# Pair stage of an attention and mixture-of-experts block: layer 2 in seven PSUM banks, rows straight from the projection, one layer-3 count a batch

## Chip, cores and metric

The kernel runs on one core of one Trainium2 chip. The metric is the device time of the whole program in microseconds (us), lower is better. Before the change the median of three runs is 1792.36 us (1785.63 to 1807.71).

## The reference

The input x is 16 batches of 256 tokens of width 256. After a layer norm it goes through a sparse attention and a routed and a shared feed-forward part, and all are added to x. The stage that the change touches decides, for every pair (i, j) of tokens of a batch, how similar they are; the 25 most similar j of each i are then the only ones that i attends to:

```
h    = xn @ W1.T                                  # 128 features a token
pair = relu(h[:, :, None, :] - h[:, None, :, :] + b1)   # for each i, j: 128 values
pair = relu(einsum('bijf,gf->bijg', pair, W2) + b2)     # layer 2: 64 values
sim  = einsum('bijg,og->bijo', pair, W3)[..., 0] + b3   # layer 3: one value
sim  = 0 on the diagonal; top_idx = top 25 of each row of sim
```

All of it is in float32. The attention (32 heads of width 2) gathers keys and values of the 25 chosen tokens; the feed-forward part sends each of the 4096 tokens to 2 of 8 experts.

## The kernel before

The program has three stages. The first (until about 96 us) makes the layer norms, the projections h, q, k and v and the routing logits, batch by batch. For all batches it leaves in SBUF `h_both`: `hneg`, which is -h, and `hb`, which is h + b1, both as 128 features x 4096 tokens. The second, the pair stage (about 96 to 1408 us), is the subject. The third (to 1787 us) runs the experts and the shared part.

The pair stage has 16 batches of 32 steps (`BSTEPS`), 512 in all, numbered n. A step takes 8 tokens i of a batch against all 256 tokens j. Its parts, each in a function that an engine's program calls in order:

- **Rows** (`relu1_row` on VectorE, L1338; `relu1` on ScalarE, L1093): for each of the 8 tokens one instruction makes relu(-h[:, j] + (h + b1)[:, i]) for all 256 j, a "row" of 128 x 256. `dve_rows(s)` says how many of the 8 VectorE makes (2 to 7; 148 in a batch), the rest (108 in a batch) is ScalarE's. Rows go to `r1`, a ring of four steps: rows of step n wait for layer 2 of step n-4.
- **Layer 2** (`layer2`, L905, TensorE): the 8 rows times W2, four matmuls of 512 columns, two at a time on the two halves of the PSUM partitions; each is recorded as two instructions, so a step has 8 records. The result fills two PSUM banks. There are three such pairs of banks (0 to 5), so layer 2 of step n waits until the ReLU of step n-3 has read its pair (`r2_done`).
- **Layer-2 ReLU** (`relu2`, L1141, ScalarE): one instruction of 128 x 1024 from the two banks to `r2`, a ring of eight steps in SBUF. It waits for layer 2 of its step (`l2_done`) and, since `r2` is used again, for a layer-3 group (`l3_done`). ScalarE does the rows of step n and then the ReLU of step n-3 (`LAG`).
- **Layer 3** (`layer3`, L917, TensorE): after every second step, four matmuls of 512 columns on four partition groups; 16 groups in a batch add into bank 6 (`ps_sim`). Each group increments `l3_done`.

VectorE takes the finished sums at step 5 of the next batch (`take_sims`, L1454), finds the top 25 in four rounds (steps 6 to 10 of each half batch) and does the attention's arithmetic between the rows. GpSimd (POOL) gathers keys and values with indirect DMAs (L734) whose turns are paced by `l2_done`. ScalarE makes the exponentials (L1145), two a batch.

The rows don't read `h_both` in place. At step 17 (`COPY`) of each batch VectorE copies the next batch's 2 x 256 columns to one of two SBUF buffers `h_now` (`copy_batch`, L1329), and at step 20 (`MOVE`) ScalarE copies the -h half of it on into PSUM bank 7 (`move_next`, L1128). ScalarE's rows of batches 1 to 15 read -h from there, and those of batch 0 from `h_now` in SBUF; VectorE's rows always read `h_now`.

The order of work on each engine is written out by hand; semaphores alone tie the engines together. SP (the DMA queue of the sync engine) waits for the last copy (`batch_copied`, in batch 14) and then loads the first experts' weights (L547 to L553) over `h_both`; POOL splits those of expert 0 (L742, L744) after its gathers in batch 15. The third stage starts with transposes (`transpose_slots`, L961) into banks 7 and 4, then 6 and 7 in turn.

Of the kernel before, what the change touches and what calls it, by code (L numbers as in the profile page):

```python
# [5 lines left out]
def lsn_attention_moe_block(  # L6
# [24 lines left out]
    ALU = mybir.AluOpType  # L31
    ACT = mybir.ActivationFunctionType
    AX = mybir.AxisListType.X
    ds = bass.ds
# [53 lines left out]
    with ctx:  # L88
# [73 lines left out]
        h_now = [part(2 * S, 2), sb("h_now1", [P, 2, S])[:, :, :]]  # L162
        hneg_now, hb_now = ([h[:, k:k + 1, :].rearrange("p o n -> p (o n)") for h in h_now] for k in range(2))
# [112 lines left out]
        ps_before = ps[:, 7, 0:NT * E].rearrange("p (t e) -> p t e", e=E)  # L276
        ps_count = ps[:, 7, NT * E:2 * NT * E].rearrange("p (t e) -> p t e", e=E)
# [65 lines left out]
        batch_copied = sem("batch_copied")  # L343
        batch_moved = sem("batch_moved")
# [70 lines left out]
        COPY, MOVE = 17, 20  # L415
# [4 lines left out]


# [45 lines left out]
        def _(sp):  # L467
# [72 lines left out]
            sp.wait_ge(batch_copied, NB)  # L540
# [46 lines left out]
            for g in range(ALL):  # L587
# [6 lines left out]
                if g == SWUG_LOAD:  # L594
                    sp.wait_ge(l3_done, NB * GROUPS)
# [231 lines left out]
        def _(pe):  # L827
# [61 lines left out]
            def count_choices():  # L889
# [3 lines left out]
                nc.tensor.matmul(ps[:, 7, 0:NT * E], earlier[:, :], hv, start=True, stop=True)  # L893
                nc.tensor.matmul(ps[:, 7, NT * E:2 * NT * E], ones[:, :], hv, start=True, stop=True).then_inc(counts_ready, 1)

            def layer2(n):
# [3 lines left out]
                if n >= PS2:  # L900

                    pe.wait_ge(r2_done, n - PS2 + 1)
                for u in range(2):
                    for v in range(2):
                        last = nc.tensor.matmul(ps_l2(n)[v * G2:(v + 1) * G2, u, :], w2t[:, :],  # L905
# [3 lines left out]
            def layer3(b, q):  # L909
# [6 lines left out]
                for c in range(4):  # L916
                    last = nc.tensor.matmul(ps[32 * c:32 * c + 32, 6, :], w3win[:, at:at + 32],  # L917
                                            r2[:, (2 * q + c // 2) % R2, 512 * (c % 2):512 * (c % 2) + 512],
                                            start=(q == 0), stop=(q == GROUPS - 1))
                last.then_inc(l3_done, 1)  # L920
# [146 lines left out]
        def _(act):  # L1067
# [13 lines left out]
            def relu1(b, i, s, first):  # L1081
# [4 lines left out]
                if s == 0:  # L1086
# [700 lines left out]
```

## Time and profile before

| | us |
|---|---|
| runs | 1807.71, 1785.63, 1792.36 |
| profiled execution, its time | 1788.49 |
| span from its first to its last instruction | 1786.8 |
| TensorE busy in the span | 1664.4 (93%) |
| VectorE busy | 1523.8 (85%) |
| ScalarE busy | 1441.1 (81%) |
| GpSimd busy | 1125.6 (63%) |
| mean granted TensorE clock | 0.991 |

The profiled execution lies 4 us under the median of the runs. Busy shares are averages over three stages; matmul ends are modelled, so that busy time of TensorE (PE) is not time at its peak. A wait is shown as idle time before an instruction, with what ended it; "remote" (or "another core or an unknown queue") stands where the profile finds no event that fits. Starts of neighbouring instructions in a timeline give what one costs its engine; the recorded duration is longer, since the end of one lies over the start of the next.

### The profile page before, as it was taken

The page shows a single profiled execution, that of the slowest core. Times are in us where ns is not written, and L with a number is a line of the kernel's source. Part 1 is how long each engine was busy: PE and PEld are TensorE (multiplying, and loading weights), DVE is VectorE, ACT ScalarE, POOL GpSimd, SP SyncE. Part 2 cuts the span into 40 slices and gives each one's busy share as a digit, 9 for nine tenths or more (in the row PEclk, how much of TensorE's full clock was granted, in tenths as well). Part 3 has the DMA queues.
Part 4 walks back from the last instruction along what each step waited for, and adds up shares of the span by engine and source line. Part 5 has one row for each costly group of instructions (what it writes and reads, how often), then busy time and mean ns, then how long its engine had stood idle before and what let it go on. Part 6 is the DMA issues. An engine that isn't in the chain of part 4 may idle for free.

```text
span 1786.8 us, 30738 instructions
## 1 busy us (share of the span) xinstructions
PE 1664.4 (93%) x9092; PEld 722.8 (40%) x9092; DVE 1523.8 (85%) x4205; ACT 1441.1 (81%) x2787; POOL 1125.6 (63%) x1027
## 2 busy tenths in 40 slices
PE   7999979999998999899999999998999999998998
PEld 6732212222222222222222222222222599997887
DVE  6898948979998998889899898998899688867888
ACT  5699948989998999899899989998899787843342
POOL 3207766767676777767676767777676634455556
PEclk9999979999999999999999999999999999999999
DMA  5622111111111111111111111111121166532333
GB/s 184 249 83 82 54 51 42 45 45 48 45 49 39 50 45 46 47 43 51 42 48 45 49 42 48 49 44 48 52 82 40 57 196 211 172 125 72 118 118 106
DMA packets 80074, 136.88 MB, mean 77 GB/s; under 512 B 22336, under 2 KB 46528, under 8 KB 79936
## 3 DMA queue, kind: packets, MB, share of 16 engines
q0 software_dynamic: 31744, 69.27, 14.0%
q1 hardware_dynamic: 48192, 65.91, 11.1%
q8 instruction: 70, 1.15, 0.3%
q14 instruction: 68, 0.56, 0.1%
HBM read 95.24 MB, written 39.85 MB: 76 GB/s over the span
## 4 chain that ended last, share of the span: by engine, by line
PE 36%; ACT 36%; DVE 9%; issue 8%; another core or an unknown queue 4%; DMA 0%; SPq 0%; ACTq 0%; DVEq 0%
ACT arena L1093 21%; PE ps L905 16%; PE ps L944 16%; ACT arena L1141 13%; DVE arena L1338 4%; PE ps L917 4%; PE ps L961 1%; DVE arena L1512 1%; ACT arena L1145 1%; DVE idx L1469 1%; DVE top L1462 0%; DVE hTs_low L1694 0%; DVE arena L1482 0%; DVE arena L1468 0%
## 5 line engine op out<-in xcount | busy, mean ns | idle before, releaser
L734 POOL DMA_INDIRECT arena<-kv_rows,gidx x800 | 887.2, 1109 | 437.8 <-issue 226.2
L905 PE MATMUL ps<-arena,w2t 128*64 128x512 f32 x4096 | 982.5, 603 | 86.5 <-ACT arena L1141 51.1
L1141 ACT ACTIVATE arena<-ps,b 128x1024 f32<-128x1024 f32 x512 | 633.9, 1242 | 133.7 <-remote 90.2
L905 PEld LDWEIGHTS ps<-arena,w2t 128*64 128x64 f32 x4096 | 281.2, 136 | 777.9 <-issue 668.7
L1338 DVE TENSOR_SCALAR arena<-h_now 128x256 f32<-128x256 f32 x1184 | 388.1, 384 | 78.1 <-remote 45.2
L1338 DVE TENSOR_SCALAR arena<-arena 128x256 f32<-128x256 f32 x1184 | 377.1, 375 | 53.1 <-PE ps L905 26.5
L1093 ACT ACTIVATE arena<-ps,h_now 128x256 f32<-128x256 f32 x864 | 382.1, 632 | 0.0
L1093 ACT ACTIVATE arena<-ps,arena 128x256 f32<-128x256 f32 x756 | 326.5, 600 | 0.0
L917 PE MATMUL ps<-arena,w3win 128*32 128x512 f32 x2048 | 275.7, 606 | 1.4 <-issue 1.2
L917 PEld LDWEIGHTS ps<-arena,w3win 128*32 128x32 f32 x2048 | 40.8, 108 | 211.1 <-issue 162.9
L1512 DVE TENSOR_TENSOR arena<-arena 128x1152 f32<-128x1152 f32 (+4 forms) x160 | 100.2, 626 | 0.4
L815 POOL DMA_INDIRECT arena<-slot_outputs,slot_get x64 | 70.3, 1099 | 29.1 <-issue 16.6
L687 POOL DMA_INDIRECT slot_inputs<-arena,slot_put x36 | 39.5, 1098 | 63.7 <-issue 48.5
L1253 ACT ACTIVATE off_diag<-ps 128x512 f32<-128x512 f32 (+1 forms) x24 | 14.3, 595 | 77.7 <-PE ps L944 36.6
L944 PE MATMUL ps<-xTe_high,wug_high 128*112 128x256 f32 (+1 forms) x240 | 70.6, 294 | 0.0
L944 PE MATMUL ps<-xT_high,swug_low 128*128 128x512 f32 x176 | 69.1, 393 | 1.3 <-issue 1.3
L944 PE MATMUL ps<-xT_high,swug_high 128*128 128x512 f32 x176 | 70.0, 398 | 0.2 <-DVE off_diag L1688 0.2
L944 PE MATMUL ps<-xT_low,swug_high 128*128 128x512 f32 x176 | 69.2, 393 | 0.0
L944 PE MATMUL ps<-xTe_low,wug_high 128*112 128x256 f32 (+1 forms) x240 | 67.5, 281 | 0.0
L944 PE MATMUL ps<-xTe_high,wug_low 128*112 128x256 f32 (+1 forms) x240 | 67.3, 281 | 0.0
L1482 DVE TENSOR_TENSOR arena<-arena,qao 128x1600 f32<-128x1600 f32 x32 | 58.3, 1822 | 6.9 <-issue 5.1
L663 POOL TENSOR_TENSOR arena<-arena 128x2 f32<-128x2 f32 x32 | 23.9, 763 | 62.1 <-DVE arena L1302 62.1
(158 smaller groups left out, 2115.7 us busy)
## 6 DMA issues: line engine op xcount, KB each, us to landing
arena<-kv_rows,gidx POOLq DMA_INDIRECT x800
slot_inputs<-arena SPq DMA_DIRECT2D x16, 640.0 KB, 3.9
arena<-slot_inputs SPq DMA_DIRECT2D x40, 256.0 KB
slot_outputs<-arena SPq DMA_DIRECT2D x40, 256.0 KB
arena<-in_L_attn_x_dram SPq DMA_DIRECT2D x16, 256.0 KB, 3.0
xn_rows<-arena SPq DMA_DIRECT2D x16, 256.0 KB, 3.8
arena<-in_L_attn_x_dram SPq DMA_DIRECT2D x8, 512.0 KB
arena<-xn_rows SPq DMA_DIRECT2D x8, 512.0 KB
```

The lines of the kernel that those rows point to most:

```text
L663: nc.gpsimd.tensor_tensor(rstd[:, r, :], veps[:, r, :], neg_half, ALU.pow).then_inc(rstd_ready[r], 1)
L687: pool.indirect_dma_start(out=slot_dram, out_offset=bass.IndirectOffsetOnAxis(ap=slots, axis=0), in_=rows, in_offset=None, bounds_check=SL ...
L734: pool.indirect_dma_start(out=kvg[:, h, r, :], out_offset=None, in_=kv_dram, in_offset=bass.IndirectOffsetOnAxis(ap=gidx[:, h, r:r + 1], a ...
L815: pool.indirect_dma_start(out=ys[c % 2][:, n, k, :], out_offset=None, in_=yslot_dram, in_offset=bass.IndirectOffsetOnAxis(ap=slot_get[:, c ...
L905: last = nc.tensor.matmul(ps_l2(n)[v * G2:(v + 1) * G2, u, :], w2t[:, :], r1[:, n % R1, 4 * u + 2 * v:4 * u + 2 * v + 2, :], start=True, s ...
L917: last = nc.tensor.matmul(ps[32 * c:32 * c + 32, 6, :], w3win[:, at:at + 32], r2[:, (2 * q + c // 2) % R2, 512 * (c % 2):512 * (c % 2) + 512],
L944: mm = nc.tensor.matmul(to, weights[a], moving[b], start=(first and i == 0), stop=(last_one and i == 2))
L1093: last = nc.scalar.activation(r1[:, n % R1, k, :], hneg_now[i] if first else ps_hneg[i], ACT.Relu, bias=hb_now[i][:, at:at + 1])
L1141: nc.scalar.activation(r2[:, n % R2, :].rearrange("p (u n) -> p u n", u=2), ps_l2(n), ACT.Relu, bias=b2[:, 0:1]).then_inc(r2_done, 1)
L1338: row = nc.vector.tensor_scalar(r1[:, (b * BSTEPS + s) % R1, k, :], hneg_now[i], hb_now[i][:, at:at + 1], 0.0, ALU.add, ALU.max)
L1482: nc.vector.tensor_tensor(prod, kvg[:, h, :, 0:KD], qao[:, ds(t, 1), :].to_broadcast([P, TOPK, KD]), ALU.mult)\
L1512: nc.vector.tensor_tensor(pve[:, 0:n, :], pve[:, 0:n, :], pve[:, rows - n:rows, :], ALU.add).then_inc(attn_step, 1)
```

## The change

Three things change in the pair stage, and three places follow from them. Layer 2 takes its banks from a table: steps 0 to 15 use three pairs as before, and from step 16 on a step's two halves take the next two of seven banks (0 to 6) in turn. A half waits only for the ReLU that last read its own bank, and the half that is free earlier goes first. Where the two banks are not neighbours (6 and 0), the ReLU is two instructions of 512 columns. The sums move to bank 7. Rows read `h_both` in place, and only the last batch is copied, once, since the experts' weights land on the original. Layer 3 increments `l3_done` once a batch, and the ReLU no longer waits for it. SP waits for the last copy and for the rows of batch 14 before it loads weights. The first transposes use banks 0 and 2.

```diff
-        h_now = [part(2 * S, 2), sb("h_now1", [P, 2, S])[:, :, :]]
-        hneg_now, hb_now = ([h[:, k:k + 1, :].rearrange("p o n -> p (o n)") for h in h_now] for k in range(2))
+        h_last = part(2 * S, 2)
...
-        PS2 = 3
-
-        def ps_l2(n):
-            return ps[:, 2 * (n % PS2):2 * (n % PS2) + 2, :]
-
-        ps_hneg = [ps[:, 7, i * S:(i + 1) * S] for i in range(2)]
-
-        ps_sim = ps[:, 6, :].rearrange("p (h n) -> p h n", h=HALVES)
+        SIM, RING2 = 7, 7
+
+        def l2_banks(n):
+
+            if n < STEPS:
+                return (2 * (n % 3), 2 * (n % 3) + 1)
+            half = 2 * (n - STEPS) + 2
+            return tuple(sorted((half % RING2, (half + 1) % RING2)))
+
+        l2_free, bank_user = [], {}
+        for n in range(NB * BSTEPS):
+            l2_free.append([bank_user.get(k, -1) + 1 for k in l2_banks(n)])
+            bank_user.update({k: n for k in l2_banks(n)})
+
+        def ps_l2(n, u):
+            return ps[:, l2_banks(n)[u], :]
+
+        ps_sim = ps[:, SIM, :].rearrange("p (h n) -> p h n", h=HALVES)
...
         def ps_xt(g):
-            bank = (7, 4)[g] if g < 2 else 6 + g % 2
+            bank = (0, 2)[g] if g < 2 else 6 + g % 2
...
+        def h_rows(b, k):
+
+            h = h_both[:, k:k + 1, b * S:(b + 1) * S] if b < NB - 1 else h_last[:, k:k + 1, :]
+            return h.rearrange("p o n -> p (o n)")
...
-            sp.wait_ge(batch_copied, NB)
+            sp.wait_ge(last_copied, 1)
+            sp.wait_ge(r1_dve, (NB - 1) * BSTEPS)
+            sp.wait_ge(r1_act, (NB - 1) * BSTEPS)
...
                 pe.wait_ge(r1_dve, n + 1)
                 pe.wait_ge(r1_act, n + 1)
-                if n >= PS2:
-
-                    pe.wait_ge(r2_done, n - PS2 + 1)
-                for u in range(2):
+                for u in sorted(range(2), key=lambda u: l2_free[n][u]):
+                    if l2_free[n][u]:
+
+                        pe.wait_ge(r2_done, l2_free[n][u])
                     for v in range(2):
...
-                last.then_inc(l3_done, 1)
+                if q == GROUPS - 1:
+                    last.then_inc(l3_done, 1)
...
-                if g == 1:
-
-                    pe.wait_ge(r2_done, NB * BSTEPS - 2)
+                if g < 2:
+
+                    pe.wait_ge(r2_done, NB * BSTEPS - 3 + g)
                 if g == 2:
+
+                    pe.wait_ge(r2_done, NB * BSTEPS)
+                if g == 3:
 
                     pe.wait_ge(sim_taken, NB)
...
-                    last = nc.scalar.activation(r1[:, n % R1, k, :], hneg_now[i] if first else ps_hneg[i], ACT.Relu,
-                                                bias=hb_now[i][:, at:at + 1])
+                    last = nc.scalar.activation(r1[:, n % R1, k, :], h_rows(b, 0), ACT.Relu, bias=h_rows(b, 1)[:, at:at + 1])
...
-            def move_next(b, i, first):
-
-                act.wait_ge(batch_copied, b + 2)
-                if first:
-                    act.wait_ge(route_done, 1)
-                nc.scalar.activation(ps_hneg[1 - i], hneg_now[1 - i], ACT.Copy).then_inc(batch_moved, 1)
...
-                if n >= R2:
-
-                    act.wait_ge(l3_done, (n - R2) // 2 + 1)
-                nc.scalar.activation(r2[:, n % R2, :].rearrange("p (u n) -> p u n", u=2), ps_l2(n), ACT.Relu, bias=b2[:, 0:1]).then_inc(r2_done, 1)
+                low, high = l2_banks(n)
+                pair = r2[:, n % R2, :].rearrange("p (u n) -> p u n", u=2)
+                if high == low + 1:
+                    nc.scalar.activation(pair, ps[:, low:high + 1, :], ACT.Relu, bias=b2[:, 0:1]).then_inc(r2_done, 1)
+                else:
+                    for u in range(2):
+                        last = nc.scalar.activation(pair[:, u, :], ps_l2(n, u), ACT.Relu, bias=b2[:, 0:1])
+                    last.then_inc(r2_done, 1)
...
-            def copy_batch(b, i):
-
-                nc.vector.tensor_copy(h_now[i], h_both[:, :, ds(b * S, S)]).then_inc(batch_copied, 1)
+            def copy_last():
+
+                nc.vector.tensor_copy(h_last, h_both[:, :, (NB - 1) * S:NB * S]).then_inc(last_copied, 1)
...
-                row = nc.vector.tensor_scalar(r1[:, (b * BSTEPS + s) % R1, k, :], hneg_now[i], hb_now[i][:, at:at + 1], 0.0, ALU.add, ALU.max)
+                row = nc.vector.tensor_scalar(r1[:, (b * BSTEPS + s) % R1, k, :], h_rows(b, 0), h_rows(b, 1)[:, at:at + 1], 0.0, ALU.add, ALU.max)
```

## Rows read from the trace of the kernel before

**Rows 1.** The page, part 1: busy us, share of the span, instructions of each engine.

```profile
PE 1664.4 (93%) x9092; PEld 722.8 (40%) x9092; DVE 1523.8 (85%) x4205; ACT 1441.1 (81%) x2787; POOL 1125.6 (63%) x1027
```

**Rows 2.** Windows, batches 0, 1, 2-14, 15: us, then PE, PEld, DVE, ACT, POOL busy us.

```profile
96.31:171.22 74.91, 72.94 (x374) 20.09 (x375) 67.89 (x283) 74.49 (x142) 28.60 (x24) 1.00 0.20 69
171.22:271.39 100.17, 84.47 (x387) 20.80 (x383) 68.77 (x187) 71.28 (x141) 69.79 (x66) 0.90 0.17 53
...
271.39:1332.49 1061.10, 991.76 (x4994) 261.75 (x4994) 952.18 (x2759) 960.05 (x1861) 752.90 (x677) 1.00 0.17 48
1332.49:1408.30 75.81, 74.96 (x387) 19.70 (x384) 62.67 (x194) 72.38 (x139) 47.14 (x41) 1.00 0.14 37
```

**Rows 3.** Timeline of TensorE, late batch 15: start us, us, engine, line, operation.

```profile
1378.88 3.65 PE L905 MATMUL ps<-arena,w2t 128*64 128x512 f32 x16
...
1383.46 3.65 PE L905 MATMUL ps<-arena,w2t 128*64 128x512 f32 x16
```

**Rows 4.** Timeline of ScalarE, batch 7: a ReLU, six rows from PSUM, a ReLU.

```profile
748.69 1.20 ACT L1141 ACTIVATE arena<-ps,b 128x1024 f32<-128x1024 f32 x1
749.69 2.39 ACT L1093 ACTIVATE arena<-ps,h_now 128x256 f32<-128x256 f32 x6
751.83 1.26 ACT L1141 ACTIVATE arena<-ps,b 128x1024 f32<-128x1024 f32 x1
```

**Rows 5.** Timeline of ScalarE, batch 14: the copy into PSUM and an exponential.

```profile
1300.45 0.51 ACT L1128 ACTIVATE ps<-h_now 128x256 f32<-128x256 f32 x1
1300.76 1.24 ACT L1141 ACTIVATE arena<-ps,b 128x1024 f32<-128x1024 f32 x1
...
1330.77 1.18 ACT L1145 ACTIVATE arena<-arena 128x800 f32<-128x800 f32 x1
1331.53 0.78 ACT L1093 ACTIVATE arena<-ps,h_now 128x256 f32<-128x256 f32 x1
```

**Rows 6.** Waits in 94 to 1411 us: who <- whom: us in total, times, longest.

```profile
PE ps L905 <- ACT arena L1141: 51.1, 70, 3.8
...
ACT arena L1141 <- remote: 90.2, 36, 16.8
```

**Rows 7.** Timelines of TensorE, ScalarE and VectorE at a pause in batch 4.

```profile
450.34 1.94 PE L905 MATMUL ps<-arena,w2t 128*64 128x512 f32 x8
...
452.89 2.46 ACT L1093 ACTIVATE arena<-ps,arena 128x256 f32<-128x256 f32 x6
457.02 1.11 ACT L1141 ACTIVATE arena<-ps,b 128x1024 f32<-128x1024 f32 x1 [1.67 <-remote]
...
457.03 0.35 DVE L1338 TENSOR_SCALAR arena<-arena 128x256 f32<-128x256 f32 x1 [0.30 <-remote]
```

**Rows 8.** The chain of waits by line: batches 2 to 14, then batch 15.

```profile
by line: ACT arena L1093 30.8%; PE ps L905 19.5%; ACT arena L1141 18.1%; issue 10.3%; DVE arena L1338 5.6%; another core or an unknown queue 5.1%; PE ps L917 4.7%; DVE arena L1512 1.1%; ACT arena L1145 0.7%; DVE idx L1469 0.7%; DVE top L146
...
by line: PE ps L905 43.9%; ACT arena L1093 22.6%; ACT arena L1141 13.8%; PE ps L917 11.8%; issue 6.2%; another core or an unknown queue 2.0%; ACTq L1140 0.1%
```

**Rows 9.** Timeline of ScalarE, batch 0: five rows from SBUF, then a ReLU.

```profile
100.64 2.09 ACT L1093 ACTIVATE arena<-arena 128x256 f32<-128x256 f32 x5
102.64 1.09 ACT L1141 ACTIVATE arena<-ps,b 128x1024 f32<-128x1024 f32 x1
```

**Rows 10.** Timeline of TensorE, batch 5: two of its waits for the ReLU.

```profile
569.02 1.94 PE L905 MATMUL ps<-arena,w2t 128*64 128x512 f32 x8 [1.15 <-ACT arena L1141]
...
595.51 1.94 PE L905 MATMUL ps<-arena,w2t 128*64 128x512 f32 x8 [0.89 <-ACT arena L1141]
```

**Rows 11.** Line L1329, the copies: duration ns min/median/max, first and last start us.

```profile
L1329 DVE COPY arena<-arena x8: 406/412/421, 93.0 to 1205.9; 128x512 f32<-128x512 f32 x8
```

**Rows 12.** Waits in batches 2 to 14 (271.39 to 1332.49 us).

```profile
ACT arena L1141 <- remote: 68.0, 33, 4.7
```

**Rows 13.** Timelines of SP and GpSimd: loads of expert weights, their split.

```profile
1291.78 0.41 SPq L547 DMA_DIRECT2D arena<-in_L_ffn_w_up_gate_dram  x1
...
1409.02 0.77 POOL L742 CAST wug_high<-arena 128x704 fp32r<-128x704 f32 x1 [1.79 <-DMA arena<-kv_rows,gidx]
```

More of the change, by code:

```diff
@@ L594, in _ @@
                 if g == SWUG_LOAD:
-                    sp.wait_ge(l3_done, NB * GROUPS)
+                    sp.wait_ge(l3_done, NB)
                 if SWUG_LOAD <= g < SWDN_LOAD and (g - SWUG_LOAD) % 2 == 0:
@@ L892, in count_choices @@
                 hv = hots.rearrange("p t e -> p (t e)")
-                nc.tensor.matmul(ps[:, 7, 0:NT * E], earlier[:, :], hv, start=True, stop=True)
-                nc.tensor.matmul(ps[:, 7, NT * E:2 * NT * E], ones[:, :], hv, start=True, stop=True).then_inc(counts_ready, 1)
+                nc.tensor.matmul(ps[:, 6, 0:NT * E], earlier[:, :], hv, start=True, stop=True)
+                nc.tensor.matmul(ps[:, 6, NT * E:2 * NT * E], ones[:, :], hv, start=True, stop=True).then_inc(counts_ready, 1)
             def layer2(n):
@@ L1079, in keep_first, with relu1 @@
                 nc.scalar.activation(xT1[:, :, ds(b * S, S)], ps_t1, ACT.Copy).then_inc(xT1_kept, 1)
-            def relu1(b, i, s, first):
+            def relu1(b, s):
                 n = b * BSTEPS + s
@@ L1085, in relu1 @@
                     act.wait_ge(l2_done, n - R1 + 1)
-                if s == 0:
-                    act.wait_ge(batch_copied, b + 1)
-                    if not first:
-                        act.wait_ge(batch_moved, b)
+                if n == 0:
+                    act.wait_ge(h_saved, START + 2)
+                if b == NB - 1 and s == 0:
+                    act.wait_ge(last_copied, 1)
                 for k in range(dve_rows(s), STEP_ROWS):
                     at = step_rows(s)[k]
-                    last = nc.scalar.activation(r1[:, n % R1, k, :], hneg_now[i] if first else ps_hneg[i], ACT.Relu,
-                                                bias=hb_now[i][:, at:at + 1])
+                    last = nc.scalar.activation(r1[:, n % R1, k, :], h_rows(b, 0), ACT.Relu, bias=h_rows(b, 1)[:, at:at + 1])
                 last.then_inc(r1_act, 1)
@@ L1105, in keep_second @@
                 for s in range(ahead):
-                    relu1(0, 0, s, True)
+                    relu1(0, s)
                 act.wait_ge(h_ready, b + 1)
@@ L1150, in _ @@
                     if n >= ROWS_AHEAD:
-                        relu1(b, b % 2, s, b == 0)
-                    if s == MOVE and b < NB - 1:
-                        move_next(b, b % 2, b == 0)
+                        relu1(b, s)
                     if n == 9:
@@ L1524, in _, with pair_batch @@
             TAKE, TOP = 5, 6
-            def pair_batch(b, i, done):
-                dve.wait_ge(batch_copied, b + 1)
+            def pair_batch(b, done):
+                if b == NB - 1:
+                    dve.wait_ge(last_copied, 1)
                 for s in range(0 if done else ROWS_AHEAD, BSTEPS):
@@ L1539, in pair_batch @@
                     for k in range(dve_rows(s)):
-                        relu1_row(b, i, s, k)
+                        relu1_row(b, s, k)
                         if k == 0:
-                            if s == COPY and done < 3:
-                                copy_batch(b + 1, 1 - i)
+                            if s == COPY and b == NB - 2:
+                                copy_last()
                             if topk and s == TAKE:
@@ L1579, in pair_batch @@
                                 scale(summed)
-            pair_batch(0, 0, 0)
-            pair_batch(1, 1, 1)
+            pair_batch(0, 0)
+            pair_batch(1, 1)
             for b in range(2, NB - 1):
-                pair_batch(b, b % 2, 2)
-            pair_batch(NB - 1, 1, 3)
+                pair_batch(b, 2)
+            pair_batch(NB - 1, 3)
             def split_low(parts, high_done, done, low_done):
```

21 lines of the change are left out of this document (9 added, 12 removed).

## Prediction

> **What bounds the kernel now.** I read the page's busy table first, then the stage by windows, then one engine's timeline at a time, then the chain of waits. The busy table says TensorE 93%, VectorE 85%, ScalarE 81% of a span of 1786.8 us [rows 1]; no engine is alone. The pair stage is 96 to 1408 us, 16 batches. Batch 0 takes 74.91 us and ScalarE is busy 74.49 of it; batches 2 to 14 take 1061.10 us, 81.6 each, with TensorE, VectorE and ScalarE busy 991.76, 952.18 and 960.05 us, and batch 15 takes 75.81 us [rows 2]. Batch 1 takes 100.17 us with one long halt at a low granted clock; I leave it as it is.
>
> What would TensorE need alone? Where nothing holds it, near the end of batch 15, two steps (16 layer-2 records and one layer-3 group) start 4.58 us apart [rows 3]: 2.29 a step, 73.3 a batch of 32 steps. What would ScalarE need? In batches from 1 on, a row starts 2.14/6 = 0.356 us after the one before, a layer-2 ReLU takes 1.00 until the next start [rows 4]. A batch has 108 ScalarE rows, 32 ReLUs and two exponentials (0.76 each, [rows 5]): 38.4 + 31.9 + 1.5 and the copy into PSUM 0.31 [rows 5], together 72.1. So TensorE and ScalarE both need 72 to 73 us and a batch takes 81.6. The missing 8 us is in two kinds of waits. TensorE waits for the layer-2 ReLU 70 times, 51.1 us in all; ScalarE waits 90.2 us "remote" [rows 6]. The first kind is the three-pair ring: the layer 2 of step n needs ReLU n-3, and ScalarE does that after its rows of step n, so TensorE starts 1.15 us after the rows were ready. The second kind is a pause, about four times in each of batches 2 to 14: ScalarE stops from 455.35 to 457.02, VectorE starts again with it, and both wait for the layer-2 count, although TensorE's record of the step asked for (450.34, 1.94 us long) had ended 4.7 us before [rows 7]. I can't say from the trace why that count comes late. In the chain of waits of batches 2 to 14 the ScalarE rows have 30.8%, the ReLUs 18.1%, layer 2 19.5% [rows 8].
>
> **The change, part by part**, against the profiled run (1788.5 us; the median of three is 1792.4, 4 above it).
>
> *Rows read SBUF in place of PSUM.* 15 batches x 108 = 1620 ScalarE rows change source. Batch 0 has the price: its rows read SBUF, and five start 2.00 us before the next ReLU, 0.400 each [rows 9], against 0.356. That is 0.044 x 1620 = 71 us more ScalarE work, 4.7 a batch. How much is on the path? In batches 2 to 14 the chain holds 0.308 x 1061 = 327 us of rows, of 13 x 38.4 = 499 us: 65%. So 0.65 x 1404 x 0.044 = 40 us; in batch 15, 22.6% of 75.8 is 17.1 of 38.4 us [rows 8]: 2 us more. **+42**, bounds 0 and +71. VectorE's rows read SBUF before and after: 0.
>
> *Seven banks in place of three pairs.* The first half of a step now needs ReLU n-4, only the second half ReLU n-3. A half step is 4 of the 8 records, 3.65/4 = 0.91 us [rows 3]. A wait up to that long goes: of the two shown (1.15 and 0.89 us, [rows 10]) the first keeps a quarter. Of 51.1 us I take 46: **-46**. Bounds -51 and 0 (if the rows of step n become what is late next). The semaphore waits on TensorE's own queue rise by one a step; each sits on a weight load, and behind it are only that step's matmuls and the layer-3 group.
>
> *Split ReLUs.* From step 16 on, one step in seven has its banks 6 and 0: 71 steps with two 512-column ReLUs. From 1.00 us for 1024 and 0.356 for 256 columns [rows 4], a column costs 0.84 ns and an instruction 0.141 us; 71 x 0.141 = 10 us. ReLUs are on the chain for 192 of 416 x 1.00 us, 46%: **+5**, bounds 0 and +10.
>
> *Copies.* 15 copies into PSUM go (0.31 us each [rows 5]; 4.6 us of ScalarE, 65% on the path: **-3**, bounds -5 and 0). 16 VectorE copies of 0.41 us [rows 11] become one; VectorE's rows have only 5.6% of the chain [rows 8]: **-1**, bounds -6 and 0. The rows no longer wait for either.
>
> *Layer-3 counts.* 240 of 256 increments and ScalarE's wait on them go; that wait asks for a group four steps older than the layer 2 it needs anyway. The 4.58 us pitch, with an increment in each group, shows no price [rows 3]: 0, bounds -6 and 0. The Trainium skill (TensorE: Matmul & The Clock Gate, "The cost: per-tile semaphore tail") has increments serialise at about 26 ns each; by it an estimate is -6 us. No row here shows such a tail.
>
> *Pauses.* ScalarE's "remote" waits in batches 2 to 14 are 33, 68.0 us [rows 12]. With TensorE up to half a step (0.91) further on, ScalarE finds more work before it stops; I take half of that each time: 33 x 0.45 = **-15**. Bounds -68 and 0; I lean to the near end because their cause isn't seen.
>
> *Expert weights.* SP's first loads move from 1291.8 us [rows 13] to when the rows of batch 14 are done, about 1329. POOL, which splits them, comes to it after its gathers, at 1409.02 [rows 13]: some 75 us of cover are left: 0. The slot loads and everything behind them on SP move with it but are first needed after 1408. If the cover went, the cost would be the landing of a few us. The transposes' banks change and wait for ReLUs that are three and two steps old: 0, bounds 0 and +2.
>
> Sum: +42 - 46 + 5 - 3 - 1 - 15 = -18, so 1788.5 - 18 = **1770 us**.
>
> **Rivals.** *A: the pauses go too and ScalarE is the bound.* Its batch is 43.2 (108 x 0.400) + 31.9 + 1.5 + 0.6 (4.6 splits) = 77.2 us. 13 batches: 1004 against 1061, -57; batch 15 +1.4. That is 1733 us; with a remaining microsecond of waits a batch, 1746. For it: batch 0 ran with three pairs, with ScalarE busy 99% and no pause. Against: the pauses come at nearly the same steps of each batch, with batch 0's PSUM ring, so the ring alone doesn't make them. The Trainium skill (Perfetto Trace Analysis, "Optimization Strategy") takes a gap that repeats for too few SBUF or PSUM buffers; by that reading this rival is the case, and the 8 us a batch would go. The rows leave it open: the pause is on the count's way to ScalarE, not on a bank.
>
> *B, slower: the pauses stay whole and the dearer rows lie wholly on the path.* ScalarE idles 1061.1 - 960.1 = 101 us in 13 batches, 7.8 each, all while it waits for the layer-2 count. If its work grows and that idle time stays, a batch is 77.2 + 7.8 = 85.0 against 81.6: +44, batches 1 and 15 about +9: 1842 us. TensorE's waits then only turn from "ReLU" into "rows". It decides where the row price on the path (42 to 71) passes what the ring and the pauses give back (46 and 15). For it: half the chain is ScalarE already, and it is ScalarE that gets 4.7 us a batch more. Against: TensorE needs only 73.3 and can run closer behind.
>
> *C: nothing happens.* TensorE's wait for ReLU n-3 is only moved to the rows of step n, worth what they cost: 1788 to 1795. For it: the rows end just 1.15 us before those starts (a ReLU of 1.00 lies between).
>
> **How the numbers follow.** Forecast case 0.45 (1755 to 1785), A 0.28, B 0.17, C 0.10. About 2% (36 us, the distance to 1756 and 1828 from the median) is what a measurement tells from no change. Faster by more: A and a tenth of the forecast case, 0.33; slower by more: B and a little, 0.20; within: 0.47. The range goes from A's bound, 1730, to most of B, 1838. Batch 1's halt (some 20 us) may fall away or come twice; that is inside it.
>
> **What would show it.** Rows at 0.400 us pitch in all batches; 71 pairs of 128x512 ReLUs; TensorE's idle time for L1141 well under 20 us; ScalarE busy over 76 us of each batch; a batch near 80 us. If the "remote" waits of ScalarE are gone, A holds; if they keep 5 us a batch with a pitch above 82, B. The prediction would be wrong if SBUF rows cost other than 0.044 more beside the attention's work, or if the late counts belong to the layer-3 increments.

## The result, and the profile after

The changed kernel takes 1821.57 us, median of 5 runs (1813.07 to 1824.33), against 1792.36 (1785.63 to 1807.71, 5 runs): a ratio of 1.014, interval 1.010 to 1.018. I had forecast 1770. The sign was wrong; the measured time lies inside the range. Ratios and their intervals compare undisturbed runs alone, so they need not be the quotient of the two medians shown. The profiled execution took 1813.07 us, 24.6 more than that of before (1788.5).

The page after, part 1 and the clock row (compare [rows 1]):

```profile
PE 1689.6 (93%) x9092; PEld 708.5 (39%) x9092; DVE 1516.0 (84%) x4190; ACT 1500.4 (83%) x2843; POOL 1148.7 (63%) x1027
...
PEclk9999979999999999999899998999899999999999
```

ScalarE has 59 us more work, VectorE 8 less, and the clock row has three new 8s. The windows of batches 0, 1, 2 to 14 and 15, as in [rows 2]:

```profile
96.60:170.20 73.60, 72.81 (x375) 20.04 (x376) 67.15 (x277) 73.42 (x142) 28.26 (x24) 1.00 0.20 68
170.20:269.90 99.70, 84.87 (x388) 20.95 (x386) 71.14 (x191) 76.75 (x146) 70.00 (x67) 0.90 0.18 54
269.90:1353.60 1083.70, 1015.45 (x4995) 248.86 (x4993) 945.14 (x2752) 1009.97 (x1906) 772.00 (x676) 0.98 0.17 45
1353.60:1433.00 79.40, 76.05 (x387) 18.87 (x384) 60.81 (x190) 77.49 (x146) 52.14 (x41) 1.00 0.21 59
```

ScalarE is busy 77.7 us of a batch (73.9 before), as foreseen. I call a stop with TensorE's clock at half behind it for 6.8 us or more a halt, and the shorter stops of [rows 7] pauses. Cut by the starts of layer 2, ten of the thirteen batches take 79.5 to 83.5 us, 81.7 on average, about before's (81.6 over all thirteen, 81.4 without batch 3, which has a halt of its own). The other three (batches 9, 12 and 14) take 88.3, 89.1 and 89.6, together 22 us more. Batch 15 gives 3.6, batches 0 and 1 take 1.8 back: 24 us, the whole loss of this execution. The waits in the pair stage, against [rows 6]:

```profile
DVE arena L1351 <- remote: 84.1, 32, 14.8
ACT arena L1152 <- remote: 58.8, 27, 12.5
PE ps L920 <- issue: 52.9, 71, 2.5
PE ps L920 <- DVE arena L1351: 18.0, 21, 3.2
PE ps L920 <- ACT arena L1152: 5.4, 9, 1.5
```

The ring did to TensorE's wait for the ReLU what the prediction said: 51.1 us are 5.4. But "issue" went from 26.3 to 52.9 us and the wait for VectorE's rows from 7.8 to 18.0. TensorE's idle time before layer 2 is 79.2 us in all, against 86.5: most of the wait only got another last releaser. Of before, then after (behind the second bar: idle us, and what ended it):

```profile
L905 PE MATMUL ps<-arena,w2t 128*64 128x512 f32 x4096 | 982.5, 603 | 86.5 <-ACT arena L1141 51.1 <-issue 26.3 <-DVE arena L1338 7.8
```

```profile
L920 PE MATMUL ps<-arena,w2t 128*64 128x512 f32 x4096 | 993.2, 607 | 79.2 <-issue 52.9
```

ScalarE's "remote" waits in batches 2 to 14 fell too, from 68.0 us [rows 12] to 44.6, without a shorter batch. One of the three halts, TensorE and then ScalarE, batch 9:

```profile
858.30 1.93 PE L920 MATMUL ps<-arena,w2t 128*64 128x512 f32 x7
861.05 0.59 PE L920 MATMUL ps<-arena,w2t 128*64 128x512 f32 x1 [0.82 <-issue]
863.96 0.78 PE L920 MATMUL ps<-arena,w2t 128*64 128x512 f32 x1 [2.31 <-DVE arena L1351]
865.31 1.01 PE L920 MATMUL ps<-arena,w2t 128*64 128x512 f32 x1 [0.58 <-issue]
868.11 1.01 PE L920 MATMUL ps<-arena,w2t 128*64 128x512 f32 x1 [1.79 <-issue]
```

```profile
860.66 2.49 ACT L1112 ACTIVATE arena<-arena 128x256 f32<-128x256 f32 x6
871.11 1.11 ACT L1152 ACTIVATE arena<-ps,b 128x1024 f32<-128x1024 f32 x1 [7.95 <-remote]
```

TensorE gets one matmul every 1.4 to 2.9 us, and its clock is then granted at 0.5 (1.2 GHz) for 10.2 us: its records go from 0.59 to 1.01 us. GpSimd has been issuing indirect transfers without a wait of more than 0.31 us from 824.63 to 867.95 us, a run of 26, the last 16 of them one every 1.26 us; the two other halts also stand at the end of runs of 26. In the kernel before, runs between 262 and 1400 us were of 16 or fewer but one (27, batch 3, the only batch with a halt there). That was my first theory, G: long runs of gathers make the halts.

### The profile page after: what moved, and what is told of

The parts are those of the page before. It is cut to its first block, busy times and chain, and to the rows that moved or that the text cites. A ratio compares the mean times of both kernels' runs of the same rounds, so it can differ in the third digit from the quotient of the medians.

```text
span 1811.3 us, 30248 instructions
## 1 busy us (share of the span) xinstructions
PE 1689.6 (93%) x9092; PEld 708.5 (39%) x9092; DVE 1516.0 (84%) x4190; ACT 1500.4 (83%) x2843; POOL 1148.7 (63%) x1027
## 4 chain that ended last, share of the span: by engine, by line
PE 67%; DVE 16%; ACT 8%; issue 4%; another core or an unknown queue 3%; DMA 1%; SPq 0%; POOL 0%; POOLq 0%; ACTq 0%; DVEq 0%
PE ps L920 38%; PE ps L960 16%; PE ps L932 10%; DVE arena L1351 9%; ACT arena L1112 3%; ACT arena L1152 2%; DVE arena L1523 1%; PE ps L884 1%; PE ps L878 1%; PE ps L980 1%; ACT arena L1121 1%; DVE idx L1480 1%; DVE top L1473 1%; DVE arena L1479 1%
## 5 line engine op out<-in xcount | busy, mean ns | idle before, releaser
L749 POOL DMA_INDIRECT arena<-kv_rows,gidx x800 | 910.9, 1139 | 441.0 <-issue 231.4
L920 PE MATMUL ps<-arena,w2t 128*64 128x512 f32 x4096 | 993.2, 607 | 79.2 <-issue 52.9
L1351 DVE TENSOR_SCALAR arena<-arena 128x256 f32<-128x256 f32 x2368 | 760.6, 378 | 152.9 <-remote 84.1
L1112 ACT ACTIVATE arena<-arena 128x256 f32<-128x256 f32 x1728 | 750.7, 519 | 0.6 <-PE ps L884 0.6
L920 PEld LDWEIGHTS ps<-arena,w2t 128*64 128x64 f32 x4096 | 264.4, 137 | 798.1 <-issue 620.3
L1152 ACT ACTIVATE arena<-ps,b 128x1024 f32<-128x1024 f32 x441 | 493.8, 1120 | 86.5 <-remote 58.8
L932 PE MATMUL ps<-arena,w3win 128*32 128x512 f32 x2048 | 290.5, 612 | 8.0 <-issue 7.4
L1155 ACT ACTIVATE arena<-ps,b 128x512 f32<-128x512 f32 x142 | 89.7, 692 | 12.1 <-remote 9.5
L1513 DVE TENSOR_TENSOR arena<-arena 128x1600 f32<-128x1600 f32 x32 | 58.2, 1820 | 0.1
```

Of the source, the lines that this page charges most:

```text
L749: pool.indirect_dma_start(out=kvg[:, h, r, :], out_offset=None, in_=kv_dram, in_offset=bass.IndirectOffsetOnAxis(ap=gidx[:, h, r:r + 1], a ...
L920: last = nc.tensor.matmul(ps_l2(n, u)[v * G2:(v + 1) * G2, :], w2t[:, :], r1[:, n % R1, 4 * u + 2 * v:4 * u + 2 * v + 2, :], start=True, s ...
L932: last = nc.tensor.matmul(ps[32 * c:32 * c + 32, SIM, :], w3win[:, at:at + 32], r2[:, (2 * q + c // 2) % R2, 512 * (c % 2):512 * (c % 2) + ...
L1112: last = nc.scalar.activation(r1[:, n % R1, k, :], h_rows(b, 0), ACT.Relu, bias=h_rows(b, 1)[:, at:at + 1])
L1152: nc.scalar.activation(pair, ps[:, low:high + 1, :], ACT.Relu, bias=b2[:, 0:1]).then_inc(r2_done, 1)
L1155: last = nc.scalar.activation(pair[:, u, :], ps_l2(n, u), ACT.Relu, bias=b2[:, 0:1])
```

## The experiments

The kernel before was timed beside every group. Its own time differed a lot from one occasion to the next, and that turned out to be the key. The theories in the expectations are named there: G (runs of gathers), R, Q and Q2 (what the rows cost and the ring gives), S (ScalarE is the bound), L (gathered rows come late).

| occasion | before, us | kernels and their ratio to it |
|---|---|---|
| A (the result) | 1792 | changed 1.014 |
| B | 1673 | e1 1.018, e2 1.018, e3 1.030, e4 1.025 |
| C | 1688 | changed 1.018, e5 1.034, e6 1.035 |
| D | 1784 | changed 1.012, e7 1.001, e8 0.999, e9 1.005 |
| E | 1671 | e11 1.062, e12 1.055, e13 1.091, e5b 1.041 |
| F | 1815 | e9b 1.010, e11b 1.045 |

On A, D and F the traces have the pauses of [rows 7]; I call these occasions pausing. On B, C and E they have none: quiet. C and F were on the same chip, so this is no property of one chip.

**One part at a time, on quiet occasions.** *e1*, the changed kernel with three pairs (its first transposes then use banks 4 and 5):

```diff
-            if n < STEPS:
-                return (2 * (n % 3), 2 * (n % 3) + 1)
-            half = 2 * (n - STEPS) + 2
-            return tuple(sorted((half % RING2, (half + 1) % RING2)))
+            return (2 * (n % 3), 2 * (n % 3) + 1)
```

> The changed kernel with its layer-2 banks back in three pairs throughout (no split ReLUs, transposes on banks 4 and 5); rows from SBUF, merged waits and one layer-3 count a batch stay. Theory G (gather runs): the pauses stand at the end of unbroken runs of POOL's indirect gathers; the ring let TensorE run ahead so that the paced waits of POOL are met at once and two runs of 16 and 10 merge into one of 26, which ends in a halt of 7 to 8 us at half clock, three times in the changed kernel. With three pairs TensorE waits for ReLUs again, the merged runs become fewer than three in batches 2 to 14, and the time is 1790 to 1800. Theory R (dear SBUF rows are the loss, the ring gives something back): without the ring it gets slower than the changed kernel, 1835 to 1860. Theory Q (the ring itself costs, by splits or half-step waits): back near 1792, but without any tie to the length of POOL's runs.

*e2*, the kernel before with ScalarE's rows read from SBUF:

```diff
-                    if not first:
-                        act.wait_ge(batch_moved, b)
...
-                    last = nc.scalar.activation(r1[:, n % R1, k, :], hneg_now[i] if first else ps_hneg[i], ACT.Relu,
+                    last = nc.scalar.activation(r1[:, n % R1, k, :], hneg_now[i], ACT.Relu,
...
-                    if s == MOVE and b < NB - 1:
-                        move_next(b, b % 2, b == 0)
```

> The kernel before with one edit: ScalarE's rows of batches 1 to 15 read the projection in SBUF, and the copy into PSUM and its waits go. Theory R: 1620 rows at 0.044 us more lie on the path for two thirds or more: 1792 + 42 to 71 = 1834 to 1863. Theory G: a batch's 81.6 us are set by the gathers' pace and the pauses, and ScalarE has 7.8 us of idle time a batch to take the 4.7 us in; ScalarE's idle time falls from 7.8 to about 4 us a batch and the time is within 10 us of 1792 unless a long halt comes or goes (8 us each).

Measured: e1 1703.47 us, e2 1704.36, both 1.018 (1.013 to 1.024), some 31 us above before's 1672.82. Then both kernels unaltered.

> The changed kernel unaltered, to see it on the chip of these experiments. Theory S (ScalarE bound): where there are no pauses, ScalarE with SBUF rows is busy in 76.6 of 76.6 us a batch; nothing that the ring does for TensorE can shorten that, and its split ReLUs add 4.6 x 0.14 = 0.6 us a batch to it, 9 us in 15 batches. The changed kernel is then 0 to 10 us slower than the three-pair kernel with SBUF rows, so 1.8% to 2.4% above the kernel before. Theory Q2 (the ring gives something back): under 1.5% above. Where the chip has the pauses of 8 us a batch, the ratio is again about 1.014.

> The kernel before unaltered, for a trace from this chip. Theory S: where the same chip runs e1 and e2 with 76.6 us a batch, this one takes 74.5 us, ScalarE busy 73.8 of it, and has no pauses in batches 2 to 14: the 81.6 us of the first trace are the chip's, not the kernel's. Theory G (runs of gathers make the pauses): pauses of 1.5 us again, four a batch.

The changed kernel took 1712.39 us, ratio 1.018 (1.012 to 1.025); the one profiled execution of before 1676.05. Its three batches 10 to 12, and below it batch 10 of e2 and of the changed kernel (us, then PE, PEld, DVE, ACT, POOL busy):

```profile
864.20:937.50 73.30, 73.30 (x388) 19.50 (x386) 71.98 (x211) 73.30 (x145) 57.09 (x53) 1.00 0.19 52
937.50:1010.70 73.20, 73.20 (x386) 19.44 (x384) 73.20 (x214) 73.20 (x145) 56.73 (x52) 1.00 0.18 51
1010.70:1084.00 73.30, 73.30 (x386) 19.48 (x384) 73.30 (x212) 73.30 (x145) 57.45 (x53) 1.00 0.19 51
```

```profile
873.90:950.50 76.60, 73.84 (x387) 19.74 (x384) 72.87 (x212) 76.60 (x144) 59.93 (x51) 1.00 0.17 48
```

```profile
878.40:955.80 77.40, 74.72 (x386) 18.70 (x384) 72.68 (x211) 77.40 (x150) 58.92 (x53) 1.00 0.18 49
```

Without pauses a batch of the kernel before takes 73.28 us, over and over: the 73.3 that TensorE needs alone. In e1 and e2 it takes 76.63, in the changed kernel 77.2 to 77.4. ScalarE is shown busy without a break in all of them, in the kernel before too, so that doesn't tell which engine is the bound; what it needs is read from its starts. Of before:

```profile
915.80 2.63 ACT L1093 ACTIVATE arena<-ps,arena 128x256 f32<-128x256 f32 x6
917.94 1.49 ACT L1141 ACTIVATE arena<-ps,b 128x1024 f32<-128x1024 f32 x1
```

Of e2:

```profile
507.39 2.88 ACT L1091 ACTIVATE arena<-h_now 128x256 f32<-128x256 f32 x6
509.78 1.49 ACT L1139 ACTIVATE arena<-ps,b 128x1024 f32<-128x1024 f32 x1
```

Six rows take 2.14 us from PSUM and 2.39 from SBUF, 0.357 and 0.398 each. (The durations overlap, so pitches are read.) ScalarE's need in e2 is 108 x 0.398 + 32 x 0.99 + 1.5 = 76.2 of 76.63 us, and in before 108 x 0.357 + 32 x 0.99 + 1.5 + 0.3 = 72.0 of 73.28: with rows from SBUF it is the bound, with rows from PSUM TensorE is. The step from 76.63 (e1) to 77.3 (changed) is 0.7 us a batch, and the split ReLUs were priced at 4.6 x 0.141 = 0.65. TensorE's waits in batches 2 to 14, of e1 and then of the changed kernel, show what the ring did meanwhile:

```profile
PE ps L917 <- ACT arena L1149: 32.5, 46, 1.1
```

```profile
PE ps L920 <- issue: 17.3, 26, 1.0
PE ps L920 <- DVE arena L1351: 15.6, 23, 1.0
```

The wait for the ReLU goes to nothing, and TensorE is idle 32.9 us in place of 34.5: it waits for the next rows. So on a quiet occasion the ring gives back nothing and costs its splits. (e1 and the changed kernel ran on different occasions, but from batch 3 on the batches of each agree within 0.2 us.)

Why is the whole run only some 36 us slower (1712.4 against 1676.1), when the 13 batches 3 to 15 at 4.0 would be 52? Batches 3, 5 and 7 of the kernel before take 79.3, 79.5 and 77.0: gathered rows come late to VectorE.

```profile
366.50 1.83 DVE L1482 TENSOR_TENSOR arena<-arena,qao 128x1600 f32<-128x1600 f32 x1 [6.60 <-DMA arena<-kv_rows,gidx]
```

TensorE stops 4.28 us behind it and gets the clock at half for 3.4 us. The slower changed kernel gives the gathers time and has no such wait over 1.6 us. That is worth 16 us to it.

**POOL's gathers.** *e3* and *e4* put a wait into the changed kernel and into the one before:

```diff
+                    if r == BREAK_AT and paced:
+                        wait_alone(pool, "pool", gathered[h], b * (16 * TOPK) + 16 * (r + 1))
...
+            BREAK_AT = 12
```

> The changed kernel; POOL waits, after the 13th gather of each tile of 16 in batches 0 to 13, until those 13 have landed, so that no run of gathers is longer than about 16. Theory G: the three long halts (8 us each) go, no stretch of the pair stage after batch 1 has the clock at half, and the time is 1790 to 1797; the short pauses of 1.5 us stay or come in other places. Theory R or Q: POOL has slack, the break does nothing: 1821.

> The kernel before with the same break in POOL's gathers. Theory G: the halt of batch 1 (two runs back to back, 25 gathers, clock at half for 20 us) and the small one of batch 3 become shorter; 1770 to 1790. The other theories: no change, 1792.

(The texts have 16 gathers a tile; it is 25, so these runs still had 25 to 27.) Measured 1718.16 us (1.030) and 1714.64 us (1.025). The occasion was quiet, so nothing of theory G was tested. In e3 the break cost batches 2 to 14 nothing: they take 77.1 us on average, as in the changed kernel unaltered on C (1712 us; before was faster on B, hence the higher ratio). In e4 it made rows late, as the waits in batches 2 to 14 show; they are from its slowest run, 1739.4 us, and the other four took 1712 to 1718:

```profile
DVE arena L1485 <- DMA arena<-kv_rows,gidx: 74.3, 13, 12.4
ACT arena L1144 <- PE ps L908: 61.4, 24, 11.2
```

*e5* and *e6* leave the gathers of tiles 0 to 28 out of the kernel before and of the changed one; one plain transfer takes their place, so the attention works on other keys and values:

```diff
+                if paced or (b == NB - 2 and h == 0):
+                    if paced:
+                        pace(b, h * (ROW - TOPK) + TOPK - 1)
+                    pool.dma_start(kvg[:, h, :, :], kv_dram[0:S, :].rearrange("(p o) n -> p o n", p=P)[:, 0:1, :].to_broadcast([P, TOPK, 2 * KD]))\
+                        .then_inc(gathered[h], 16)
+                    return
```

> The kernel before with the 16 indirect gathers of each of the tiles 0 to 28 replaced by one plain transfer of the same size (so the attention's keys and values are not the gathered ones); the transfer is issued by POOL where the last gather was. Theory G: if the chip shows pauses at all, they vanish with the gathers: a batch takes 74 to 75 us instead of 81.6, and the halt of batch 1 is gone (15 us): 1670 or less where before takes 1792. Theory S: on a chip without pauses only the halt of batch 1 goes, 10 to 20 us; on one with pauses they stay.

> The changed kernel with the gathers replaced in the same way (keys and values not the gathered ones). Both theories: with no pauses left ScalarE is the bound and this is slower than e5 by 2 to 3 us a batch, 30 to 45 us in all. If instead it equals e5, the SBUF rows' price is not on the path when pauses are gone.

1738.40 (1.034) and 1739.11 us (1.035): slower, and alike. The one transfer starts where the last gather did and lands late; VectorE waits for it 134 us in 26 places of batches 2 to 14 in e5, 136 us in e6. Late rows set both times, so they say nothing of ScalarE. A miss, and a lesson: POOL's side has little slack, and "leave the work out" delayed it. A repeat (e5b) came out quiet again, 1739.49 us, 1.041.

> The kernel before without the gathers of tiles 0 to 28 once more (one plain transfer each, so keys and values are not the gathered ones), for a chip with pauses. It took 1738 us where before took 1688, since the one transfer lands 5 to 7 us late for VectorE. Theory G: on a chip with pauses it takes the same 1735 to 1745, now below before's 1785, and no 'remote' wait is left. Otherwise the pauses add to it: 1800 or more.

**On a pausing occasion (D).** *e7* moves six ScalarE rows a batch to VectorE in the changed kernel:

```diff
-            return (6, 7, 6, 3, 3, 7, 5, 4, 5, 2, 7, 6, 2, 2, 3, 6)[s % STEPS]
+            return (6, 7, 6, 3, 3, 7, 5, 4, 5, 3, 7, 6, 3, 3, 3, 6)[s % STEPS]
```

> The changed kernel with one more row on VectorE in three of every 16 steps (steps 9, 12 and 13): 102 ScalarE rows a batch in place of 108. Theory S (ScalarE is the bound because its rows got dearer): ScalarE's batch falls from 77.3 by 6 x 0.40 = 2.4 to about 75 us, VectorE's rises from 72.4 by 6 x 0.27 to 74; the time is 15 x 2.4 = 30 to 36 us below the changed kernel, about 1680. The rival (a chain of waits through the ring or the counts, not ScalarE's work, sets the 77.3): no change, or slower, since VectorE's steps with the top-8 work get longer.

> The changed kernel unaltered, for comparison with the run of rebalanced rows on the same chip. Theory S: 77.2 to 77.4 us a batch, ratio to before 1.018 to 1.024 where the chip has no pauses. Where it has them, 81 to 82 us in most batches and 1.014.

The changed kernel took 1810.35 us (1784.97 to 1841.34, four runs), 1.012 (1.004 to 1.020); e7 1788.49 us (ten runs), 1.001 (0.998 to 1.005). The medians are 22 us apart, less than the 30 to 36 of theory S. But the changed kernel's four runs lie 56 us apart, and the two faster ones average 1795, 6 us above e7: that fewer ScalarE rows bring the change back to the time of before is likely, not shown. Ordinary batches didn't move. Batches 2 to 14 of e7, then of the changed kernel's profiled execution, which was its fastest run and had one halt instead of three:

```profile
268.60:1326.40 1057.80, 1009.87 (x4994) 251.81 (x4992) 968.46 (x2815) 980.33 (x1828) 758.14 (x677) 0.99 0.17 46
```

```profile
268.60:1325.10 1056.50, 1000.34 (x4996) 249.00 (x4994) 947.32 (x2752) 1009.33 (x1906) 755.38 (x677) 1.00 0.17 46
```

81.4 and 81.3 us a batch. Without the halted ones (batches 4 and 13 of e7, batch 14 of the other) they have 80.8 and 80.9, although ScalarE has 2.4 us less to do in e7: on this occasion its work is not what sets an ordinary batch. The mean granted clock suggests that the runs differ by their halts: the changed kernel's four runs have 0.992, 0.983, 0.980 and 0.972 at 1785, 1804, 1816 and 1841 us; before's fastest 0.993 at 1777, its slowest 0.986 at 1800. One halted batch of the first trace (0.94 of the clock in 89 us, 7 us longer) costs the mean 0.003; from 1785 to 1841 us that makes, as an estimate, some seven more halts, about 50 of those 56 us.

*e8*, the kernel before with one layer-3 increment a batch:

```diff
-                last.then_inc(l3_done, 1)
+                if q == GROUPS - 1:
+                    last.then_inc(l3_done, 1)
...
-                if n >= R2:
-
-                    act.wait_ge(l3_done, (n - R2) // 2 + 1)
```

> The kernel before with the layer-3 part of the change alone: one increment a batch in place of 16, ScalarE's wait on them gone. TensorE's batch is 73.28 us, the sum of its matmuls, in both: no change, within 2 us. The rival, increments that serialise (an estimate of 26 ns each by the Trainium skill, TensorE: Matmul & The Clock Gate, 'The cost: per-tile semaphore tail'): 240 x 0.026 = 6 us less, a batch at 72.9.

1784.14 against 1783.75 us, 0.999 (0.995 to 1.003). The interval is too wide to exclude 6 us, but two steps start 4.58 us apart with 16 increments a batch [rows 3] and with one, as here in the changed kernel:

```profile
380.71 3.65 PE L920 MATMUL ps<-arena,w2t 128*64 128x512 f32 x16
384.30 1.06 PE L932 MATMUL ps<-arena,w3win 128*32 128x512 f32 x8
385.29 3.65 PE L920 MATMUL ps<-arena,w2t 128*64 128x512 f32 x16
```

*e9*, the kernel before without POOL's rests between its early scatters:

```diff
-                    rest(i * HALVES + h + 1)
```

> The kernel before without POOL's MEMSET and its wait after each pair of early scatters. Ten such pairs lie between 171 and 212 us, 2.0 us of rest each, ahead of the first gathers (from 214 us), and VectorE's first attention waits 18.5 us for their rows. Theory L (rows that come late to VectorE are what halts TensorE): the gathers start when their indices are there, 193 us, the halt of batch 1 is gone (batch 1 at 73 to 75 us in place of 91.6), and the small ones in batches 3, 5 and 7 with it: 1640 to 1660. Theory G (long runs of gathers make the halts): the halt stays or moves, 1670 or more.

1794.82 us, 1.005 (1.001 to 1.009): no gain. Batch 1 fell from 100 to 76 us, but batch 0 rose from 75 to 109. First and last of its 36 back-to-back scatters, then TensorE in the same stretch:

```profile
132.84 4.58 POOL L687 DMA_INDIRECT slot_inputs<-arena,slot_put  x1 [41.96 <-issue]
...
181.09 0.97 POOL L687 DMA_INDIRECT slot_inputs<-arena,slot_put  x1 [0.31 <-issue]
```

```profile
151.22 0.62 PE L904 MATMUL ps<-arena,w2t 128*64 128x512 f32 x1 [0.84 <-issue]
153.34 1.01 PE L904 MATMUL ps<-arena,w2t 128*64 128x512 f32 x1 [1.50 <-issue]
...
163.15 1.01 PE L904 MATMUL ps<-arena,w2t 128*64 128x512 f32 x1 [1.09 <-issue]
181.22 3.31 PE L904 MATMUL ps<-arena,w2t 128*64 128x512 f32 x8 [17.06 <-DVE arena L1337]
```

Once their rows are loaded these scatters wait for no other engine, so cause and effect can't be swapped: some 12 of them in, TensorE gets one matmul every 1.4 to 2.8 us, from 163 us nothing, and all resumes as the run ends. It is the picture of the halt in batch 9.

**Shorter runs of gathers.** *e11* and *e12* wait after the 13th and 25th gather of a tile (kernel before, changed kernel), *e13* after the 9th, 17th and 25th (before): `if r in BREAKS and paced`.

> The kernel before; POOL waits for its gathers to land after the 13th and the 25th of each tile's 25 (batches 0 to 13), so that no unbroken run of indirect transfers is longer than about 14. Four waits of 2.1 us a batch bring POOL's own cycle to 52 x 1.26 + 8.4 = 74 us. Theory G (on a chip with pauses, a run of POOL's indirect transfers of more than some 13 starves the other engines; shown so far by a run of 36 that stopped TensorE): the halts of 8 us go and the pauses get fewer; a batch takes 74 to 78 us in place of 81.6, 1690 to 1740 where before takes 1785. Theory S alone: no change on such a chip. On a chip without pauses both expect a loss, since the rows come late to VectorE: about 1.02.

> The changed kernel with the same waits. Theory G and S together: once the pauses are gone ScalarE's 77.3 us are the bound, and this is slower than e11 by 1 to 3 us a batch, 15 to 45 us in all. If it equals e11, the price of the SBUF rows is not on the path.

> The kernel before with POOL's wait for landing after the 9th, 17th and 25th gather of each tile. POOL's cycle becomes 52 x 1.26 + 12.6 = 78 us. Theory G: no pause is left, a batch is 78 us whatever the chip, and it is slower than e11 by 0 to 4 us a batch. If pauses stay at four a batch, the length of the runs is not their cause.

The occasion was quiet: 1776.69 (1.062), 1761.62 (1.055) and 1821.15 us (1.091). More breaks, later rows: in batches 2 to 14 VectorE waits for gathered rows 124.2 us in e11 and 103.3 in e12. That e12 is the faster of the two contradicts what was expected; its profiled execution has one long batch (87.5 us) where e11's has three, and I can't say why.

The last two repeat e9 and e11.

> The kernel before without the rests between its early scatters once more, for the other kind of chip. On the chip with pauses its run of 36 back-to-back scatters stopped TensorE, VectorE and ScalarE for 30 us in batch 0 and it came out 1.005. Where before has no pauses (1670 to 1690): if such starving is the chip's own, there is no halt in batch 0, the first gathers start 20 us earlier, the 18.5 us wait of batch 1 goes and with it the small waits for late rows in batches 3, 5 and 7: 1635 to 1660, faster than both kernels. If the halt of batch 0 comes here too, 1675 or more, and run length starves the engines on every chip.

> The kernel before with POOL's waits after the 13th and 25th gather once more. Where before has no pauses it is again some 6% slower (rows late for VectorE, 1777). Where before has them (about 1785), theory G expects that the halts go: not slower than before's 1785, and if late rows cost the same as on the other chip, 1777.

The occasion was pausing: e9b comes out like e9, 1834.44 us, 1.010 (1.006 to 1.014), batch 0 at 109 us again. Whether those scatters halt anything on a quiet occasion was not seen. e11b took 1895.97 us, 1.045 (1.035 to 1.055), with runs of at most 15, and its pauses got longer. In 262 to 1460 us:

```profile
ACT arena L1144 <- remote: 140.9, 37, 7.5
DVE arena L1341 <- remote: 95.6, 33, 7.6
```

So theory G falls in the form in which I held it. A long run can starve the engines, but cutting the runs doesn't take the pauses away. Nor is a run of 26 enough: behind batch 1 the changed kernel's trace on D has five runs of 25 and one of 27, and only the 27 ends in a halt.

**Where the halts begin.** Some 28 us ahead of the half clock of batch 9, one gather takes 7.69 us in place of 0.95, about as long as VectorE makes 25 rows without a gap. On D, in batch 5, the same 25 rows come with gaps, the gather beside them takes 1.83 us, and no halt follows. First the gather and VectorE ahead of the halt, then on D:

```profile
835.67 7.69 POOL L749 DMA_INDIRECT arena<-kv_rows,gidx  x1 [0.30 <-issue]
836.60 6.64 DVE L1351 TENSOR_SCALAR arena<-arena 128x256 f32<-128x256 f32 x25
```

```profile
585.28 1.83 POOL L749 DMA_INDIRECT arena<-kv_rows,gidx  x1 [0.31 <-issue]
586.18 7.83 DVE L1351 TENSOR_SCALAR arena<-arena 128x256 f32<-128x256 f32 x25
```

After the long gather GpSimd issues at its full pace, 16 in a row here, and then all engines stop. Such a pair, 18 to 25 gapless rows and a gather of 5.3 to 7.7 us, stands 27 to 31 us ahead of every halt behind batch 1 in the traces of before, of the changed kernel on A and D, and of e8, e9 and e9b; e7 has two halts without it, and not every pair is followed by a halt (the changed kernel's one on C is not). On the quiet occasion C it stands 39 to 40 us ahead of the half clock that the late rows bring in before's batches 3, 5 and 7. No run took the pair away alone, so that it is the cause isn't shown, nor why the changed kernel's first trace has more of them than before's.

No version tried beats the kernel before.

## Why the prediction was wrong

**The step that failed is the sum's return: "Seven banks in place of three pairs", -46, and with it the -15 for the pauses.** The wait I counted did go (51.1 to 5.4 us). I took it as time on the path; its bound of 0, "if the rows of step n become what is late next", was the case. On quiet occasions this is shown: with SBUF rows ScalarE needs 76.2 us of its own, above TensorE's 73.3, so nothing that lets TensorE run ahead can shorten a batch; e1's wait of 32.5 us goes, TensorE's idle time stays, and the splits cost 0.7 a batch. On the pausing occasion of the result TensorE's idle time before layer 2 fell by 7 us, not 46, and ordinary batches stayed at 81.7 us. For the pauses, ScalarE's "remote" waits shrank by 23 us, more than my 15, but the dearer rows filled that time (its busy time rose by 50), and no batch got shorter. What made this result slower, rather than equal, are the three halts (22 us), which no term of the sum had.

**SBUF rows, +42: the row's price was right, their share of the path came out near by luck.** The pitch is 0.398 against 0.357, the forecast 0.044 a row. Alone (e2, quiet) they cost 31 us: 3.35 in each of batches 3 to 15 and 1.9 in batch 2, 45 us, less the 16 us of late-row waits that disappear. I had put 65% on the path by shares of the chain; on a quiet occasion it is what ScalarE needs above TensorE's 73.3. Neither e1 nor e2 ran on a pausing occasion, so rows and ring were never told apart there; their sum is near nothing in an ordinary batch (81.7 against 81.6), and e7's 2.4 us less of ScalarE work changed it by nothing.

**Split ReLUs, +5: 0.7 us a batch** on a quiet occasion, 9 us over the pair stage, near my upper bound of 10. **Layer-3 counts, copies, expert weights, transposes:** no effect seen; SP's first load moved to 1350.65 us and nothing after the pair stage waited for it.

**Rivals.** B came nearest in mechanism, dearer rows on the path against a ring that returns little, and TensorE's waits turning into waits for rows, at 1842 us; its premise that the pauses add in full to ScalarE's work does not hold, as ordinary batches stayed at 81.7. A's batch of 77.2 us for ScalarE as the bound was right to 0.1 us (77.3), but it comes from 73.28, not from 81.6: on the quiet occasions its cure for the pauses wasn't needed. By the Trainium skill (Perfetto Trace Analysis, "Optimization Strategy") repeating gaps can mean too few buffers. Here the deeper ring left ScalarE's "remote" waits at 44.6 of 68.0 us and the batch as long as it was, and both buffer depths run without any such wait on quiet occasions, so for these gaps the measurement decides against that reading.

**What stays open.** Why the changed kernel has more halts on a pausing occasion, and what a pausing occasion is. Shown is that the halts carry its loss in the first trace. That ScalarE's load makes them is suggested by e7 (1.001) and not shown; breaking the runs of gathers in the kernel before did not help. The kernel without gathers, e1 and e2 never ran on a pausing occasion.

## What to carry to other kernels

Before a wait is counted as a gain, compute what each engine needs alone in that stage, after the change: if one needs more than the engine whose wait goes, the gain is zero, and the loss is what that engine now needs above the old bound (76.6 against 73.3 here). When a pause has no cause in the trace, price the change with and without it; a second occasion may show the other case. A transfer engine with a few us of slack a batch must be treated as a fourth bound: GpSimd's 52 transfers at 1.26 us are 65.5 of 73.3 us here.

## What the runs showed of the hardware

- The same kernel took 1671 to 1717 us on one occasion and 1800 to 1825 on another, on the same chip. The traces from a pausing and a quiet occasion differ by pauses of ScalarE, VectorE and TensorE together: a batch takes 81.6 us with them (A) and 73.28 without (C).
- On pausing occasions 36 back-to-back indirect transfers of GpSimd (1.28 us each) slowed the three engines from about the 12th on, until the run ended some 30 us later.
- A gather of GpSimd (0.95 us) took 7.69 us beside 25 rows that VectorE made without a gap, and 1.83 us beside 25 rows with gaps.
- After 4.3 us without matmuls TensorE's clock was granted at half (1.2 GHz) for 3.4 us, in the halts of batches 9, 12 and 14 for 10.2 us each, and in e9's stop of batch 0 for 30.7 us; matmul records then take 1.01 us in place of 0.59.
- The ScalarE row of 128 x 256 is 0.04 us dearer from SBUF than from PSUM, on both kinds of occasion.
